# State space scan: ten states of sixteen through TensorE's diagonals instead of eight, and the output sums issued by a table

## The reference, cut to what matters

```
decay = exp(dt[..., None] * A)
inp   = (dt * x)[..., None] * Bm[:, :, None, :]
s = dec * s + ip                       # per step, channel and state
y = einsum('bdn,bn->bd', s, c)         # sum over the 16 states
y = y + D_skip * x
```

## Time and profile before

| | |
|---|---|
| median of three runs | 4252.76 us (4248.78 to 4253.03) |
| the profiled execution's own time | 4248.74 us |
| span of its records | 4247.1 us |
| first scan to last scan of the phase | 272.1 to 1069.6 us, 256 scans |
| VectorE, TensorE, GpSimd and ScalarE busy, whole span | 79%, 83%, 32% and 54% |

### The profile page before, as it was taken

How to read it: one execution, slowest core, us unless ns; L and a number is a source line. 1 busy time by engine, 2 the same in 40 slices (tenths; PEclk the granted TensorE clock), 3 DMA queues, 4 the chain that set the end, 5 groups by cost and what they waited for, 6 DMA issues and landing times. The chain is left out here.

```text
span 4247.1 us, 65595 instructions
## 1 busy us (share of the span) xinstructions
PE 3539.1 (83%) x20079; PEld 2129.0 (50%) x20080; DVE 3364.3 (79%) x4283; ACT 2304.1 (54%) x4128; POOL 1344.3 (32%) x873
## 2 busy tenths in 40 slices
PE   8968888889549887878699999999999996469960
PEld 3445555555338777767533333333333334369950
DVE  8959999999776566645589889899998965758868
ACT  6855555555674432210048888888888882123323
POOL 4448888889103333310100000000000002744430
PEclk9979999999789988889879999999999996579985
DMA  6764444444678823247402222222222204323249
GB/s 214 257 204 159 169 164 167 161 164 139 234 234 214 226 77 94 69 114 208 129 26 66 59 65 62 61 66 58 66 58 70 53 8 118 124 71 91 90 150 300
DMA packets 534911, 536.99 MB, mean 126 GB/s; under 512 B 85168, under 2 KB 440624, under 8 KB 534496
## 3 DMA queue, kind: packets, MB, share of 16 engines
q1 hardware_dynamic: 520704, 496.18, 38.7%
q0 software_dynamic: 13952, 37.74, 2.6%
HBM read 317.41 MB, written 215.19 MB: 125 GB/s over the span
## 5 line engine op out<-in xcount | busy, mean ns | idle before, releaser
L2170 DVE TENSOR_REDUCE at_top<-at_psM 128x1 f32<-128x1024 f32 x1024 | 1206.1, 1220 | 136.6 <-PE at_psM L2021 135.8
L2130 ACT ACTIVATE at_probs<-at_psS 128x512 f32<-128x512 f32 x2048 | 1060.7, 604 | 251.1 <-PE at_psS L2047 251.0
L2047 PE MATMUL at_psS<-at_q,at_k 64*128 64x512 f32 x2048 | 795.3, 469 | 8.3 <-ACT at_probs L2130 8.3
L575 POOL TENSOR_TENSOR sc_prod<-sc_state,sc_c_row 128x1024 f32<-128x1024 f32 x256 | 708.8, 2786 | 116.8 <-DVE sc_state L724 108.5
L2021 PE MATMUL at_psM<-at_k,at_q 62*128 62x512 f32 x2048 | 689.6, 451 | 36.5 <-DMA at_vraw<-scratch_vf 21.9
L724 DVE TENSOR_TENSOR_SCAN sc_state<-sc_dec,sc_psI 128x1024 f32<-128x1024 f32 x256 | 578.6, 2280 | 53.0 <-PE sc_psI L645 28.0
L2021 PEld LDWEIGHTS at_psM<-at_k,at_q 62*128 62x128 f32 x2048 | 313.2, 190 | 601.6 <-DVE at_top L2170 519.3
L2060 PE MATMUL at_psV<-at_probs,at_v 128*32 128x512 f32 x4096 | 546.4, 605 | 0.0
L656 PE MATMUL sc_psY<-sc_prod,sc_ident 128*128 128x512 f32 x1024 | 467.3, 597 | 3.5 <-DVE sc_y L710 2.2
L606 ACT ACTIVATE sc_dec<-sc_dt,sc_a_exp 128x1024 f32<-128x1024 f32 x256 | 293.5, 1147 | 312.4 <-DVE sc_state L724 309.7
L2047 PEld LDWEIGHTS at_psS<-at_q,at_k 64*128 64x128 f32 x2048 | 337.9, 184 | 195.3 <-ACT at_probs L2130 190.8
(11 more groups left out here) (393 smaller groups left out, 5089.1 us busy)
## 6 DMA issues: line engine op xcount, KB each, us to landing
sc_c_row<-scratch_bc SPq DMA_DIRECT2D x128, 512.0 KB, 4.0
scratch_xs<-at_zeros SPq DMA_DIRECT2D x140, 264.0 KB, 4.3
sc_b_row<-scratch_bc SPq DMA_DIRECT2D x64, 512.0 KB, 5.0
ec_y<-scratch_ys SPq DMA_DIRECT2D x32, 512.0 KB, 6.6
ex_x<-scratch_xs SPq DMA_DIRECT2D x39, 264.0 KB, 3.2
si_x<-in_x SPq DMA_DIRECT2D x16, 512.0 KB, 4.4
scratch_xn<-si_xn SPq DMA_DIRECT2D x16, 512.0 KB, 5.0
scratch_x_t<-si_xT SPq DMA_DIRECT2D x16, 512.0 KB, 5.7
```

The source lines that it names most:

```text
L575: pool.tensor_tensor(prod[:, (n * H + h) % 8, :], state[slot][:], c_row[n % ROWS][:], ALU.mult).then_inc(prod_ready, 1)
L2047: pe.matmul(psS[v % 3][:], rows_of(k4[j], h, 0, GROUP)[:, c * P:(c + 1) * P], rows_of(q4[j], h, 0, GROUP)[:, half * TILE:(half + 1) * TILE ...
L2130: act.activation(probs[:, slot(j, v), :], psS[v % 3][:], ACT.Exp).then_inc(act_done, 1)
L2170: dve.tensor_reduce(top[j % 2][:, h, c:c + 1], psM[t % 2][:], AX.X, ALU.max, negate=True).then_inc(maxed, 1)
```

## The change

Six states instead of eight are mixed: 1, 4, 7, 10, 13 and 15. So ten are diagonal: 0, 2, 3, 5, 6, 8, 9, 11, 12 and 14. TensorE's adds are no longer one a step: at step `own` it issues `ADDS[state of unit own + 1]` of them, which is none to two, and the sequence of adds runs five behind at the end of a batch instead of three. The outputs of the batch before stand after units 3 and 4 instead of 2 and 3. The turn moves from steps 13 and 14 to steps 19 and 20, because the fourth mixed state is 10 instead of 7.

```diff
-    MIXED = tuple(range(1, S, 2))
+    MIXED = (1, 4, 7, 10, 13, 15)
     DIAG = tuple(n for n in range(S) if n not in MIXED)
     ND, NX = len(DIAG), len(MIXED)
-    LAG = 3
+    ADDS = (1, 2, 1, 0, 2, 1, 0, 2, 1, 0, 2, 1, 0, 1, 1, 1)
+    BEHIND = 5
...
+        added = [sum(ADDS[(before + 1) // H % S] for before in range(own)) - BEHIND for own in range(PER + 1)]
+        assert added[PER] == PER - BEHIND and all(added[own + 1] - 1 <= own - 3 for own in range(PER))
...
                             if n in DIAG:
-                                then = n + 1 if n + 1 in DIAG else n + 2
-                                if then < S:
-                                    fill(b, then, h)
+                                order = DIAG.index(n) + 1
+                                if order < ND:
+                                    fill(b, DIAG[order], h)
                                 elif place < 3:
-                                    fill(b + 1, then - S, h)
+                                    fill(b + 1, DIAG[0], h)
...
-                        if own >= LAG:
-                            add(b, own - LAG, place)
-                        elif place > 1:
-                            add(b - 1, own + PER - LAG, place - 1)
+                        for done in range(added[own], added[own + 1]):
+                            if done >= 0:
+                                add(b, done, place)
+                            elif place > 1:
+                                add(b - 1, done + PER, place - 1)
...
-                for own in range(PER - LAG, PER):
+                for own in range(PER - BEHIND, PER):
                     add(B - 1, own, 3)
...
-                        if own in (2, 3) and place > 1:
-                            output(b - 1, 1 - k, own - 2)
+                        if own in (3, 4) and place > 1:
+                            output(b - 1, 1 - k, own - 3)
```

## The result

The changed kernel takes 4271.81 us (median of 5 runs, 4268.1 to 4278.1) against 4252.76 us before. The ratio is 1.0047, with a 95% interval of 1.0032 to 1.0062: slower, by 19 us. The profiled execution took 4272.55 us, its span is 4270.9 us, 23.8 us more than the one before.

What follows compares the result with a forecast made beforehand. VectorE was taken as the bound, with TensorE the fullest engine after the change. 4248.7 us plus 9.9 for batches and end and 4.5 for clock gave 4263, plus 1 for the median 4264 us; range 4250 to 4275.

Steps and rivals of the forecast that it cites:

- Mixes to diagonals: Each batch: VectorE loses four mixes, 5.9 us, at most 47 us over the phase; TensorE gets four scan inputs, 7.5 us.
- the new cycle: Six units, two diagonal states and one mixed, repeat in 17.8 us against 17.9 before: 0.1 us gained per cycle.
- the ring: Longest dependency chain over six units, from first mixed unit's scan through TensorE's inputs and adds back to that scan: 17.8 us.
- Start of a batch: VectorE waits 0.6 to 0.7 us, then 1.4, for inputs behind adds; units 0 to 10 take 32.7 us, before 32.0.
- Turn (of u): Around VectorE's wait for the copy of u: six units take 20.2 us, no change counted, 0.5 either way.
- end of a batch: State 13 has one add a step, so TensorE stands at input 28: a gap of about 3.4 us in every batch.
- Batches 0 and 7: Their cycle was shorter before, 17.4 us for six units, against 17.5 or 17.6 through TensorE: +1.4 and +2.0 us.
- Clock: TensorE's gap lowers its clock in nearly every batch: 7 drops in place of 4, 1.5 us each, +4.5 us.
- The turns stay: The holes on TensorE at the loop's turns, about 1.6 us each, keep their cost.
- GpSimd holds the mix: Rival: mixes find a product just begun and wait up to 1.15 us more; 24 us, 4285 us; chance 0.10.
- TensorE keeps up: Rival: inputs and adds run tighter, cycle 17.4 us or less, 4247 us down to 4210; chance 0.09.
- The same without the clock's price: Rival: clock drops stay at four or fewer or cost little; 4255 us; chance 0.27.

Runs made afterwards that it cites:

- e5: Changed kernel with one add at every step, three behind, outputs after units 2 and 3, as in the kernel before: ratio 1.0045 to the kernel before.
- e3: Changed kernel with batches 1 to 6 as straight code, no loop: 4276.56 us, ratio 0.9997 to the kernel before.
- e7: Changed kernel in straight code, one add moved from state 2's entry to state 13's... see ADDS (1,1,1,0,2,1,0,2,1,0,2,1,0,2,1,1), three behind, outputs after units 2 and 3: ratio 0.9930.
- e9: Kernel before, its eight mixed states kept, in straight code with adds (1,1,0,2) for states 0 to 3, outputs after units 3 and 4: ratio 0.9944.
- e12: Changed kernel with one add per step moved from state 2 to state 15, gap before input 28 kept: ratio 1.0040 to the kernel before.
- e2: Changed kernel with 16 semaphore increments on TensorE and 16 on VectorE ahead of the first batch: ratio 1.0026 to the kernel before.
- e1: Changed kernel with one add per step moved from state 2 to state 13: 4276.19 us, ratio 0.9995 to the kernel before.
- e6: Changed kernel with one add per step moved from state 1 to state 13: 4277.03 us, ratio 0.9992 to the kernel before.
- e4: Kernel before with batches 1 to 6 as straight code, no loop: 4267.66 us, ratio 0.9973 to the kernel before.
- e10: Changed kernel with 16 semaphore increments on VectorE only, ahead of the first batch: ratio 1.0039 to the kernel before.

## Why the prediction was right or wrong

The median came at 4271.8 where 4264 was said, in the range, and slower, as the likeliest case had it. But the move is 19 us where 11 were forecast, and the parts of the sum fit worse than the whole: the batches and the end were put 4.4 us too high, while 10.2 us at the loop's turns were left out. That the two errors have opposite signs, and with them that the time lies well inside the range, is in part luck. In the terms of the prediction the profiled execution moved by 5.5 us for batches and end (9.9 said), 5.5 for the clock (4.5 said), 10.2 for the turns (none said) and 2.55 behind the phase (none said), 23.8 in all.

- *Mixes to diagonals, the new cycle*: right. 17.70 us were measured against 17.8 by the ring. VectorE's work fell by 31 us, less than the 47 that were the bound from above; it is busy 90.8 to 91.0 us in a batch where 89 was said, in part because the longest mix at the turn of u takes 2.98 us instead of 2.37. e5 shows that the order of TensorE's work sets the waits, e3 that the cycle without the loop equals TensorE's own sum, and the windows of e7 and e9 that the fullest engine changes. But the reason given for 1.78 against 1.88, that the second of two inputs is shorter, is wrong: the tenth comes with an input that waits for a scan. In e3, where none does, single inputs behind adds have 1.78 too.
- *Start of a batch*: right in size and place. Waits of 0.72 and 1.22 us (0.6 to 0.7 and 1.4 said), and 32.7 us for the first ten units, as said. What it missed is that they aren't a separate cost: e12 shows that, with the gap kept, relief here is paid again at the end of the batch.
- *Turn (of u), end of a batch*: right. The gap of 3.4 us was measured at 3.15 to 3.33. A batch without a disturbance is 100.2 us where 100.65 was said, so +0.4 instead of +0.8 for each, 2.4 instead of 4.8.
- *Batches 0 and 7*: mis-sized. +1.4 and +2.0 were said; without its drop batch 0 is 97.6 against 96.9 us, and batch 7 is 93.5 (measured so in e3) against 92.9, so +1.4 in all. With 1.85 us for the end, where 1.7 was said, the term of +9.9 comes to some 5.5.
- *Clock*: about right. Six drops behind the gap where seven were said, at 1.9 us on average instead of 1.5, 11.3 us. The four before cost 5.8, so +5.5 instead of +4.5. The slow clock behind the turns is counted with the turns.
- *"The turns stay"*: this is the step that failed. They cost 13.4 us instead of 3.2. The prediction had the row for it and treated it as a constant, though nothing said that a hole in which an engine waits for its own instructions would keep its length when the code around it changes. e2 shows that it doesn't (7.0 us after a shift alone), and in e3 the holes are gone.
- 2.55 us in the phases behind the scan are not explained. e12, on a chip where the kernel before takes about the same time, has 3167.0 us there, so it may be spread between executions; it wasn't tested.

Of the rivals, *GpSimd holds the mix* did not occur, though the mean of a mix, 1417 ns after 1332, is over the 1.33 us that were named as a sign of it. It rose because one of the two mixes at the turn of u waits longer (2.98 instead of 2.37 us) and they are now two in twelve and not two in sixteen; those in the cycle take 1.44 and 1.21 us. *TensorE keeps up* did not occur: the cycle is above 17.4, and the pair of inputs at 3.57 us was already in the bounds. *The same without the clock's price* comes near to what e1 and e6 then made true by another table.

## What to carry to other kernels

When work is moved from the fullest engine to one that is nearly as full, sum both engines over the repeating cycle first; if they come out alike, as they did here, there is little to gain in the cycle, and the time is in the holes of the new bound. Here a hole on the bounding engine was paid even where nothing waited for it then, and on TensorE it may be paid again as clock; so look at the edges of the pattern, not at its middle. In a hand-written order inside a loop, price the loop's turn as part of the change: compare with the same code written out straight before judging the edit itself.

## What the runs showed of the hardware that I had not expected

- A wait for code at a loop's turn changes with the code ahead of the loop and in it. In the changed kernel TensorE stopped 2.2 us ahead of the first input and another 2.2 us after 3 of its records; 16 instructions on TensorE and VectorE ahead of the loop took the second stop away (13.4 to 7.0 us for two turns). e5 and e12, whose tables differ, have one stop at each turn without any shift (2.1 to 2.5 us), e1 and e6 two; straight code (e3, e4, e7, e9) has none. The two engines' waits for code overlap: taking VectorE's 3.59 us away alone won nothing at the turn.
- Of 40 gaps of 3.15 to 3.33 us on TensorE (the changed kernel, e2, e3, e10 and e12) 30 were followed by a drop of the clock. So were four of the eight gaps of 2.0 to 2.25 us in the kernel before and six of the seven of 2.1 us in its straight form. In e7 and e9, whose gaps stay below 1.55 us after the start of the phase, there is no drop.
- A float32 scan input takes 1.88 us when it starts within 0.06 us of the end of the scan that it waits for, and 1.78 us otherwise, behind an add as behind another input.
- From a mix to the scan that reads it, on VectorE, 1.40 us pass in the loop and 1.24 us in straight code.
